# Attention of one layer: scores of stacked bf16 parts, computed a second time transposed and less their maximum, instead of transposed probabilities

## The chip, the cores and the metric

The kernel runs on one core of a Trainium2 chip. The metric is the device time of one execution in microseconds (us). The engines are PE (TensorE), DVE (VectorE), ACT (ScalarE), POOL (GpSimd) and SP, which issues DMAs; ACT issues some too.

## The reference

A gated cross attention and then a gated mixture of experts, for 16 batches of 128 rows of 256 features:

```
x = x + tanh(g_xattn) * xattn(layernorm(x), ctx, ctx)      # 16 heads of 16, causal
x = x + tanh(g_ffn) * experts(layernorm(x))                # 32 experts x 4 sets

Q, K, V = q @ Wq.T, k @ Wk.T, v @ Wv.T                     # split in heads
scores = where(causal, Q K^T, -inf) / sqrt(16)
out = (softmax(scores) V) @ Wo.T + bo

logits = grouped rows of 32 . controller, + ramp; perm = (logits == max over the rows)
out = perm^T (relu(perm rows . f1 + bias) . f2)
```

The factors on Wq and Wk make the scores large, and the routing compares for equality, so the attention is computed at nearly full float32 precision.

## The kernel before

Everything is in one program with hand-placed semaphores; each engine's instructions stand in the order in which its block writes them. There are three stages: attention over the 16 batches, routing (`route`) over the 16 batches, and the experts with the weighted return (`expert_in`, `expert_out`, `transpose_y`, `combine`).

In attention, a batch has four chunks of four heads (`HC` = 4, `NC` = 4), `attend` runs over them, and I call one chunk's turn on PE a slot. In a slot PE adds the causal mask in bf16 (L340) and the scores in float32 (L344), in four 32-column tiles of the array; weighs V with the transposed probabilities of three slots ago (L360, `weigh_v`); transposes the probabilities of two slots ago (L351, `transpose_p`); and does one piece of the projections: K (L320), the output rows (L330) with the transposes of x (L313), Q (L320), and V (L330). L330 multiplies a high and a low part in three products; L320 is plain float32, which PE executes as two passes. DVE takes the row maximum (L908), ACT the exponential per head with its sum (L673), DVE the reciprocal (L857), POOL scales the probabilities (L261), and ACT and DVE by turns copy the transposed probabilities (L638, L870). PE works two and three slots behind, so POOL's product is not waited for in the steady state. `bass.ds` and `Fori` are loops of the program; batches 3 to 14 are in them.

At the start DVE takes the statistics of the first four batches (L820), then 13 steps for the reciprocal deviation (`rstd`), and normalizes (L839). SP loads the context, x and the first 16 of 32 experts' weights (`wx`, a ring of `RING` = 16) before the loop; the other 16 are loaded while the experts run, each when a place is free.

## Time and profile before

| | us |
|---|---|
| median of 3 runs | 319.41 (316.90 to 321.29) |
| profiled execution | 319.98 |
| its span, first to last instruction | 318.2 |
| first scores on PE | 18.4 |
| last residual of attention | 203.5 |
| routing, to the first expert on PE | 237.2 |
| experts, to the first transpose of the return | 282.2 |

The stretches are read from the order of time of the instructions. 1.8 us of the execution lie outside the span. The profile gives a granted clock of PE as a share of 2.4 GHz: 1.00 is 2.4 GHz and 0.50 is 1.2 GHz. Lengths of single matmuls overlap, since they are pipelined; distances between their starts are what PE spends.

### The profile page before, as it was taken

The page shows a single profiled execution, that of the slowest core. Times are in us where ns is not written, and L with a number is a line of the kernel's source. Part 1 is how long each engine was busy: PE and PEld are TensorE (multiplying, and loading weights), DVE is VectorE, ACT ScalarE, POOL GpSimd, SP SyncE. Part 2 cuts the span into 40 slices and gives each one's busy share as a digit, 9 for nine tenths or more (in the row PEclk, how much of TensorE's full clock was granted, in tenths as well). Part 3 has the DMA queues.
Part 4 walks back from the last instruction along what each step waited for, and adds up shares of the span by engine and source line. Part 5 has one row for each costly group of instructions (what it writes and reads, how often), then busy time and mean ns, then how long its engine had stood idle before and what let it go on. Part 6 is the DMA issues. An engine that isn't in the chain of part 4 may idle for free.

```text
span 318.2 us, 9488 instructions
## 1 busy us (share of the span) xinstructions
PE 286.0 (90%) x3472; PEld 223.0 (70%) x3472; DVE 212.5 (67%) x531; ACT 190.8 (60%) x722; POOL 107.8 (34%) x140
## 2 busy tenths in 40 slices
PE   2195899999999999999999997789988899979995
PEld 2153667778887877777877766667767789867773
DVE  1965997988788887878787984899964233212222
ACT  2035677777777777777777785278764233234553
POOL 4114345544554554455445555145510000000000
PEclk9999999999999999999999997799999755559999
DMA  6992000000000000000000000000005640001222
GB/s 199 369 388 88 2 19 19 19 1 20 16 16 0 16 16 16 0 16 16 13 4 0 0 2 2 0 1 2 0 0 180 214 144 2 6 0 52 72 75 70
DMA packets 12362, 16.52 MB, mean 52 GB/s; under 512 B 1200, under 2 KB 7728, under 8 KB 12336
## 3 DMA queue, kind: packets, MB, share of 16 engines
q1 hardware_dynamic: 11472, 14.83, 14.2%
q10 hardware_dynamic: 864, 1.33, 1.3%
q8 instruction: 17, 0.28, 0.4%
q14 instruction: 9, 0.07, 0.1%
HBM read 14.06 MB, written 2.10 MB: 51 GB/s over the span
## 4 chain that ended last, share of the span: by engine, by line
PE 69%; DVE 13%; SPq 5%; issue 5%; DMA 3%; ACT 3%; POOL 1%; DVEq 0%; ACTq 0%; POOLq 0%
PE banks L351 10%; PE banks L344 9%; PE banks L360 9%; PE banks L562 8%; PE banks L590 7%; PE banks L320 7%; PE banks L330 7%; PE banks L545 4%; DMA cT<-in_ctxT_dram 3%; PE banks L599 3%; PE banks L340 3%; SPq L214 2%; DVE nmax L908 2%; DVE permb L897 2%; PE banks L520 1%
## 5 line engine op out<-in xcount | busy, mean ns | idle before, releaser
L673 ACT ACTIVATE pr<-banks,nmax 128x128 f32<-128x128 f32 x256 | 90.5, 369 | 24.0 <-PE banks L351 17.3
L261 POOL TENSOR_TENSOR pr<-pr,rsum 128x512 f32<-128x512 f32 x64 | 66.6, 1041 | 92.3 <-DVE rsum L857 92.1
L344 PE MATMUL banks<-kd,qz 128*32 128x128 f32 (+3 forms) x512 | 66.9, 437 | 0.0
L360 PE MATMUL banks<-pT,va 128*32 128x128 f32 x512 | 62.0, 276 | 1.7 <-ACT pT L638 1.3
L908 DVE TENSOR_REDUCE nmax<-banks 128x4 f32<-128x512 f32 x64 | 44.0, 687 | 19.5 <-PE banks L344 18.2
L673 ACT ACTIVATION_READ_ACCUMULATOR pr<-banks,nmax 128x1 f32 x256 | 53.2, 208 | 0.0
L360 PEld LDWEIGHTS banks<-pT,va 128*32 128x32 f32 x512 | 38.3, 110 | 17.5 <-DVE pT L870 2.6
L351 PE MATMUL banks<-cf,pr 128*128 128x128 f32 x256 | 42.4, 289 | 1.6 <-POOL pr L261 1.5
L351 PEld LDWEIGHTS banks<-cf,pr 128*128 128x128 f32 x256 | 27.1, 141 | 15.4 <-issue 11.5
L638 ACT ACTIVATE pT<-banks 128x512 f32<-128x512 f32 x32 | 19.2, 599 | 18.5 <-PE banks L351 18.5
L562 PE MATMUL banks<-hb,wx 32*128 32x64 f32 x512 | 27.4, 377 | 2.1 <-ACT hb L751 1.0
L562 PEld LDWEIGHTS banks<-hb,wx 32*128 32x128 f32 x512 | 24.9, 280 | 4.5 <-issue 2.6
L756 ACT ACTIVATE routed<-banks 128x512 f32<-128x512 f32 x16 | 9.6, 598 | 30.0 <-PE banks L562 30.0
L1042 DVE COPY routed<-banks 128x512 f32<-128x512 f32 x16 | 11.1, 692 | 23.8 <-PE banks L562 23.8
L772 ACT ACTIVATE ys<-banks 128x1024 f32<-128x1024 f32 x16 | 16.7, 1043 | 16.0 <-PE banks L590 16.0
L590 PEld LDWEIGHTS banks<-cf,routed 128*128 128x128 f32 x128 | 20.9, 251 | 7.2 <-issue 6.2
L1054 DVE SCALAR_TENSOR_TENSOR xs<-banks,tg,xs 128x256 f32<-128x256 f32 x16 | 7.7, 484 | 26.1 <-PE banks L599 26.1
L590 PE MATMUL banks<-cf,routed 128*128 128x128 f32 x128 | 24.0, 337 | 0.8 <-ACT routed L756 0.8
L320 PE MATMUL banks<-cT,w 128*128 128x128 f32 x128 | 18.5, 290 | 6.6 <-ACT cTh L645 6.0
L839 DVE TENSOR_SCALAR xn<-xs,mv,rs 128x256 f32 (+1 forms) x32 | 23.8, 743 | 0.0
L870 DVE COPY pT<-banks 128x512 f32<-128x512 f32 x32 | 22.0, 688 | 1.6
L320 PEld LDWEIGHTS banks<-cT,w 128*128 128x128 f32 x128 | 16.7, 204 | 8.4 <-DMA w<-in_wattn_dram 5.9
(89 smaller groups left out, 525.2 us busy)
## 6 DMA issues: line engine op xcount, KB each, us to landing
wx<-in_wexp_dram SPq DMA_DIRECT2D x32, 256.5 KB, 5.9
cT<-in_ctxT_dram SPq DMA_DIRECT2D x16, 128.0 KB, 2.1
xs<-in_x_dram SPq DMA_DIRECT2D x4, 512.0 KB, 10.7
out_dram<-xs SPq DMA_DIRECT2D x16, 128.0 KB, 1.7
w<-in_wattn_dram ACTq DMA_DIRECT2D x4, 256.0 KB, 8.0
cf<-in_constf_dram ACTq DMA_DIRECT2D x1, 148.0 KB, 5.9
gb<-in_gbo_dram ACTq DMA_DIRECT2D x1, 129.0 KB, 7.9
ctrl_in<-in_ctrl_dram SPq DMA_DIRECT2D x1, 128.0 KB, 10.5
```

The lines of the kernel that those rows point to most:

```text
L261: pool.tensor_tensor(pr[:, c % 2], pr[:, c % 2], rsum[:, c * HC:(c + 1) * HC, None].to_broadcast([P, HC, P]), ALU.mult)\
L320: last = pe.matmul(dst[:, o * P:(o + 1) * P], weight[:, i, o * P:(o + 1) * P], src[:, i, :], start=(i == 0), stop=(i == KH - 1))
L330: last = pe.matmul(dst[:, 0:E], stationary, moving, start=(q == 0), stop=(q == len(parts) - 1))
L344: last = pe.matmul(bs[r, :, 0:(j + 1) * DP], qz[:, k, c // 2, c % 2, r], kd[:, k, c // 2, :, 0:(j + 1) * DP], start=False, stop=True, tile ...
L351: last = pe.transpose(BT[:, j * P:(j + 1) * P], pr[:, c % 2, j, :], ident)
L360: last = pe.matmul(BO[k][j * DP:(j + 1) * DP, o:o + P], va[:, k, c * HC + j, D * (1 - odd):][:, 0:DP], pT[:, c % 2, j * P:(j + 1) * P], st ...
L562: last = pe.matmul(bank[4 + s][:, o:o + GROUPS], wx[s * F:(s + 1) * F, e % RING, KH * P + h * P:KH * P + (h + 1) * P], hb[s * F:(s + 1) * ...
L590: last = pe.transpose(BY2[k][g // 2][:, o:o + P], routed[:, h, :, b * NG + g], ident)
L673: last = act.activation(pr[:, c % 2, j, :], BS[c % 2][:, j * P:(j + 1) * P], ACT.Exp, bias=nmax[:, c * HC + j:c * HC + j + 1], accum_out=p ...
L839: dve.tensor_scalar(xn[:, k, :], xs[:, b, :], mv[:, b, 0:1], rs[:, bass.ds(b, 1)], ALU.subtract, ALU.mult).then_inc(ready, 1)
L870: dve.tensor_copy(pT[:, c % 2, :], BT[:, :]).then_inc(pT_ready_dve, 1)
L908: dve.tensor_reduce(nmax[:, c * HC:(c + 1) * HC], BS[c % 2][:, :].rearrange("p (j t) -> p j t", j=HC), AX_X, ALU.max, negate=True).then_in ...
```

## The change

Q and K are projected for two batches at a time (a group), each in three products of high and low parts, with the weights' columns reordered by dimension. Each result is split in three bf16 parts (ACT, DVE, ACT, POOL), written to DRAM (`keep_rows`), and read back by three DMAs (`stack`) as a stack of 96 rows per head, six combinations of parts, so that one bf16 matmul over 96 rows gives the scores. The scores are computed twice: once as before (`scores`), from which DVE takes the row maximum alone, and six slots later transposed (`scores_less_max`), with three more rows that hold the three bf16 parts of the negative maximum (`split_max`, `spread_max`, `place_max`, three small DMAs per batch) against rows of ones. ACT takes one exponential over 512 columns, and the result is already what `weigh_v` needs. The transposes, the scaling on POOL and the copies are gone; `weigh_v` also multiplies with ones, which gives the sums, and DVE divides afterwards (`weigh_out`). The mask is added by one 512-column bf16 matmul for each of the two kinds of scores. The program of attention and routing is written out without loops. The tiles of attention share their memory with `wx` and `routed`, so all 32 experts' weights are loaded after the last residual (`x1_ready`, NB). The experts' instructions are otherwise the same.

```diff
+            def keep_rows(rows, parts, g, mid, low, kept):
+                sp.wait_ge(mid, g + 1)
+                sp.wait_ge(low, g + 1)
+                sp.dma_start(rows[g].rearrange("t r c -> r t c"), parts[:, :, :]).then_inc(kept, 16)
+            def stack(st, rows, g, order, kept, stacked):
+                sp.wait_ge(kept, 16 * (g + 1))
+                if g >= STACKS:
+                    sp.wait_ge(t_done, 2 * NC * (g - STACKS + 1))
+                at = 0
+                for lo, hi in order:
+                    n = (hi - lo) * D
+                    sp.dma_start(st[at:at + n, g % STACKS].rearrange("p h b c -> p (h b c)"),
+                                 rows[g, lo:hi].rearrange("t (d h) c -> (t d) (h c)", d=D)).then_inc(stacked, 16)
+                    at += n
...
+            def stack_q(g):
+                stack(qst, q_rows, g, ((0, 3), (0, 2), (0, 1)), q_kept, q_stacked[g % STACKS])
+            def stack_k(g):
+                stack(kst, k_rows, g, ((0, 3), (1, 3), (2, 3)), k_kept, k_stacked[g % STACKS])
...
+            load_x(0)
+            load_context(0)
+            load_context(1)
+            for i in range(1, NB // XC):
+                load_x(i)
             sp.dma_start(ctrl_in[:, :, :], ctrl).then_inc(small_loaded, 16)
-            for r in range(RING):
-                sp.dma_start(wx[:, r], wexp[r]).then_inc(wx_loaded[r], 16)
-            with sp.Fori(1, NB // 2) as i:
-                b = i * 2
-                for k in range(2):
-                    sp.wait_ge(c_ready, b + (k - 1))
-                    sp.wait_ge(k_done, b + (k - 1))
-                    sp.dma_start(cT[:, k], ctxT[b + k]).then_inc(ctx_loaded[k], 16)
-            for e in range(RING, NE):
-                sp.wait_ge(e_done, (e - RING) // 2 + 1)
-                sp.dma_start(wx[:, e - RING], wexp[e]).then_inc(wx_loaded[e - RING], 16)
-            with sp.Fori(0, NB // 2) as i:
-                b = i * 2
-                for k in range(2):
-                    sp.wait_ge(yo_ready, b + (k + 1))
-                    sp.dma_start(out[b + k], xs[:, b + k, :]).then_inc(stored, 16)
+            keep_k(0)
+            stack_k(0)
+            load_context(2)
+            keep_q(0)
+            stack_q(0)
+            load_context(3)
+            keep_k(1)
+            keep_q(1)
+            stack_k(1)
+            stack_q(1)
+            for g in range(NG2):
+                if 1 <= g < NG2 - 1:
+                    keep_q(g + 1)
+                    stack_q(g + 1)
+                if g + 2 < NG2:
+                    keep_k(g + 2)
+                    stack_k(g + 2)
+                if g + 4 < NG2:
+                    load_context(g + 4)
+            sp.wait_ge(x1_ready, NB)
+            for e in range(NE):
+                sp.dma_start(wx[:, e], wexp[e]).then_inc(wx_loaded[e], 16)
...
+            pool.affine_select(causal.rearrange("p (j t) -> p j t", j=HC), causal.rearrange("p (j t) -> p j t", j=HC),
+                               [[0, HC], [-1, P]], ALU.is_ge, NEG, base=0, channel_multiplier=1)
+            pool.affine_select(causalT.rearrange("p (j q) -> p j q", j=HC), causalT.rearrange("p (j q) -> p j q", j=HC),
+                               [[0, HC], [1, P]], ALU.is_ge, NEG, base=0, channel_multiplier=-1)\
+                .then_inc(masks_ready, 1)
...
+            def project_k(g, o, to):
+                if o == 0:
+                    pe.wait_ge(c_ready, g + 1)
+                project(to, K, cTh[:, g % CR], cTl[:, g % CR], o, k_done if o == KH - 1 else None)
...
+                to = BS[n % 2]
+                pe.matmul(to[:, :], identb, causal, start=True, stop=False, skip_group_check=True)
+                for j, h in enumerate(idx):
+                    last = pe.matmul(to[:, j * P:(j + 1) * P], qst[0:SROWS, g % STACKS, h, b % 2, :],
+                                     kst[0:SROWS, g % STACKS, h, b % 2, :], start=False, stop=True,
+                                     skip_group_check=True)
                 last.then_inc(s_done, 1)
...
+            def scores_less_max(n):
...
+                    pe.wait_ge(rows_loaded[b % 2], 48 * (b // 2 + 1))
+                if n >= 2:
+                    pe.wait_ge(p_ready, n - 1)
+                to = BT[n % 2]
+                pe.matmul(to[:, :], identb, causalT, start=True, stop=False, skip_group_check=True)
+                for j, h in enumerate(idx):
+                    last = pe.matmul(to[:, j * P:(j + 1) * P], kst[0:TROWS, g % STACKS, h, b % 2, :],
+                                     qst[0:TROWS, g % STACKS, h, b % 2, :], start=False, stop=True,
+                                     skip_group_check=True)
+                last.then_inc(t_done, 1)
...
+            def spread_max(b):
+                pe.wait_ge(np_ready, b + 1)
+                if b >= 3:
+                    pe.wait_ge(x1_ready, b - 2)
+                pe.matmul(BB[0:PARTS * H, 0:P], npart[:, :, :].rearrange("p t h -> p (t h)"), identb,
+                          start=True, stop=True).then_inc(nT_done, 1)
...
+                pe.wait_ge(p_ready, n + 1)
+                window = slice(D * (1 - e), D * (1 - e) + DP)
+                for at, kind in ((0, "v"), (E, "ones")):
+                    for j in range(HC):
+                        left = va[:, b % VR, o * 8 + 4 * e + j, window] if kind == "v" else ones[:, window]
+                        last = pe.matmul(BO[b % 2][j * DP:(j + 1) * DP, at + o * P:at + (o + 1) * P], left,
+                                         pT[:, n % PR, j * P:(j + 1) * P], start=(e == 0 and at == 0), stop=(e == 1),
+                                         tile_position=(0, j * DP), skip_group_check=True)
                 last.then_inc(av_done, 1)
...
+            pe.wait_ge(w_low[K], 1)
+            for o in range(KH):
+                project_k(0, o, BA)
             pe.wait_ge(consts_loaded, 16)
-            pe.wait_ge(xn_ready, 1)
-            transpose_x(0, 0)
-            pe.wait_ge(w_loaded[1], 16)
-            pe.wait_ge(xT_ready, 1)
-            project(BQ, wq, xT, q_done)
-            pe.wait_ge(w_ready, 1)
-            pe.wait_ge(c_ready, 1)
-            pe.wait_ge(k_ready, 1)
...
+            for n in range(SLOTS_N):
+                s, g = n % 8, n // 8
+                if 0 <= n - LT < CH:
+                    if n == LT:
+                        pe.wait_ge(qr_ready, 2)
+                    scores_less_max(n - LT)
+                if n < CH:
+                    scores(n)
+                if s % 4 == 0 and 0 <= n // 4 - 1 < NB:
+                    if n == 4:
+                        pe.wait_ge(xTl_ready, 1)
+                    spread_max(n // 4 - 1)
+                if 0 <= n - LA < CH:
+                    weigh_v(n - LA)
+                if s in (1, 2) and g + 2 < NG2:
+                    if s == 1 and g >= 1:
+                        pe.wait_ge(qr_ready, g + 2)
+                    project_k(g + 2, s - 1, BA)
+                if s % 4 == 0 and 0 <= n // 4 - 1 < NB:
+                    project_v(n // 4 - 1)
+                if s == 4 and g + 2 < NG2:
+                    pe.wait_ge(kr_ready, g + 3)
+                    transpose_x(g + 2, BA)
+                if s % 4 == 2 and 0 <= (n - 14) // 4 < NB:
+                    project_out((n - 14) // 4)
+                if s in (6, 7) and g + 2 < NG2:
+                    project_q(g + 2, s - 6, BA)
+                if n == CH + 1:
+                    pe.wait_ge(max_ready, CH)
+                    transpose_r(0)
+                if n == CH + 3:
...
+            def weight_high(m):
+                act.wait_ge(w_loaded[m], 16)
+                if m in (K, Q):
+                    for j in range(2 * KH):
+                        last = act.activation(wh[:, m].rearrange("p k (o d h) -> p (k o) d h", o=KH, d=D)[:, j],
+                                              by_dim(w, m)[:, j], ACT.Copy)
+                else:
...
+            def mid_part(parts, rest, g, rest_ready, ready):
+                act.wait_ge(rest_ready, g + 1)
+                act.activation(parts[:, 1, :], rest[:, :], ACT.Copy).then_inc(ready, 1)
...
+                act.activation(pT[:, n % PR, :], BT[n % 2], ACT.Exp, scale=float(D) ** -0.5).then_inc(p_ready, 1)
+            def place_max(b):
+                act.wait_ge(nT_done, b + 1)
+                if b >= 2:
+                    act.wait_ge(rows_loaded[b % 2], 48 * (b // 2))
+                act.activation(nT[:, b % 2, :], BB[0:PARTS * H, 0:P], ACT.Copy).then_inc(nT_ready, 1)
+                act.wait_ge(nT_ready, b + 1)
+                for t in range(PARTS):
+                    act.dma_start(qst[SROWS + t:SROWS + t + 1, (b // 2) % STACKS, :, b % 2, :], nT[t * H:(t + 1) * H, b % 2, :])\
+                        .then_inc(rows_loaded[b % 2], 16)
...
+            context_high(0)
+            weight_high(K)
+            weight_high(Q)
+            k_high(0)
+            context_high(1)
+            k_mid(0)
+            xT_high(0, BB)
+            q_high(0, bank[4])
+            k_high(1, bank[5])
+            q_mid(0)
+            k_mid(1)
+            xT_high(1, bank[3])
+            weight_high(V)
+            q_high(1, bank[2])
+            q_mid(1)
+            act.wait_ge(gates_loaded, 16)
+            act.activation(tg[:, :], gates_sb[:, :], ACT.Tanh).then_inc(tanh_ready, 1)
+            context_high(2)
+            weight_high(WO)
...
+            dve.memset(kst[SROWS:TROWS], 1.0).then_inc(shift_ready, 1)
...
+            def split_max(b):
+                m, r = nmax[:, b % 2, :], nrest[:, b % 2, :]
+                dve.wait_ge(max_ready, NC * (b + 1))
+                if b >= 1:
+                    dve.wait_ge(nT_done, b)
+                dve.tensor_copy(npart[:, 0, :], m).then_inc(np_step, 1)
+                dve.wait_ge(np_step, 3 * b + 1)
+                dve.tensor_tensor(r, m, npart[:, 0, :], ALU.subtract).then_inc(np_step, 1)
+                dve.wait_ge(np_step, 3 * b + 2)
+                dve.tensor_copy(npart[:, 1, :], r).then_inc(np_step, 1)
+                dve.wait_ge(np_step, 3 * b + 3)
+                dve.tensor_tensor(npart[:, 2, :], r, npart[:, 1, :], ALU.subtract).then_inc(np_ready, 1)
...
+            def weigh_out(b):
+                dve.wait_ge(av_done, NC * (b + 1))
+                dve.reciprocal(rsum[:, :, :], BO[b % 2][:, E:2 * E].rearrange("p (h t) -> p h t", h=KH))\
+                    .then_inc(rsum_ready, 1)
+                dve.wait_ge(rsum_ready, b + 1)
+                if b >= 1:
+                    dve.wait_ge(onl_ready, b)
+                dve.tensor_tensor(on[:, :, :], BO[b % 2][:, 0:E].rearrange("p (h t) -> p h t", h=KH), rsum[:, :, :],
+                                  ALU.mult).then_inc(on_ready, 1)
...
+            normalize_x(0)
+            normalize_x(1)
+            weight_low(K)
+            weight_low(Q)
+            k_rest(0)
+            xT_low(0, BB)
+            normalize_x(2)
+            normalize_x(3)
+            q_rest(0, bank[4])
+            k_rest(1, bank[5])
+            xT_low(1, bank[3])
+            q_rest(1, bank[2])
             dve.wait_ge(gates_loaded, 16)
             dve.wait_ge(tanh_ready, 1)
             dve.tensor_scalar(bo_sb[:, :], bo_sb[:, :], tg[:, 0:1], None, ALU.mult).then_inc(bo_ready, 1)
-            split_weight(1)
-            attend(0, 0, first=True)
+            statistics(XC, NB)
+            for stage in range(RSTD_STAGES):
+                if stage == 0:
+                    rstd_ready()
...
+            for n in range(SLOTS_N):
+                s, g = n % 8, n // 8
+                if n < CH:
+                    row_max(n)
+                if s % 4 == 3 and n // 4 < NB:
+                    split_max(n // 4)
+                if s % 4 == 3 and 0 <= (n - 15) // 4 < NB:
+                    residual((n - 15) // 4)
+                if s == 0 and 2 <= g + 1 < NG2:
+                    q_rest(g + 1)
+                if s % 4 == 0 and 0 <= n // 4 - 3 < NB:
+                    weigh_out(n // 4 - 3)
+                if s in (1, 2) and g + 2 < NG2:
+                    normalize_x(2 * (g + 2) + s - 1)
+                if s == 3 and g + 2 < NG2:
+                    k_rest(g + 2)
+                if s == 5 and g + 2 < NG2:
+                    xT_low(g + 2)
+                if n == CH - 2:
+                    dve.wait_ge(stats_ready, late)
+                if CH - 2 <= n < CH + 2:
```

PE in the loop, in the steady state. Before, from the second slot of a batch to the next:

```order
L340 MATMUL banks<-cb 32x4x32 x4
L344 MATMUL banks<-kd,qz 32x4x32
L344 MATMUL banks<-kd,qz 32x4x64
L344 MATMUL banks<-kd,qz 32x4x96
L344 MATMUL banks<-kd,qz 32x512
L360 MATMUL banks<-pT,va 32x128 x4
L351 MATMUL banks<-cf,pr 128x128 x4
L320 MATMUL banks<-cT,w 128x128 x4
```

After, one slot (L504 and L506 are the scores less the maximum, L486 and L488 the plain scores, L534 `weigh_v`, L428 half of K's projection):

```order
L504 MATMUL banks<-cb 128x512
L506 MATMUL banks<-qst,kst 128x128 x4
L486 MATMUL banks<-cb 128x512
L488 MATMUL banks<-kst,qst 128x128 x4
L534 MATMUL banks<-pT,va 32x128 x4
L534 MATMUL banks<-pT,ones 32x128 x4
L428 MATMUL banks<-cTh,wh 128x256
L428 MATMUL banks<-cTl,wh 128x256
L428 MATMUL banks<-cTh,wl 128x256
L428 MATMUL banks<-cTh,wh 128x256
L428 MATMUL banks<-cTl,wh 128x256
L428 MATMUL banks<-cTh,wl 128x256
```

The transposes are gone, and the mask and the scores stand twice; `weigh_v` has twice the matmuls.

DVE at the start, after the last step of `rstd` for the first four batches (L839 normalizes, L908 is the first row maximum). Before:

```order
L839 TENSOR_SCALAR xn<-xs,mv,rs 128x256
L844 TENSOR_TENSOR kd<-banks,cf 128x512 x2
L853 COPY xT<-banks 128x256
L834 CAST wh<-w 128x512
L836 TENSOR_TENSOR wl<-w,wh 128x512
L839 TENSOR_SCALAR xn<-xs,mv,rs 128x256
L960 TENSOR_SCALAR gb<-gb,tg 128x256
L834 CAST wh<-w 128x512
L836 TENSOR_TENSOR wl<-w,wh 128x512
L908 TENSOR_REDUCE nmax<-banks 128x4
```

After (L995 sets the rows of ones, L998 normalizes, L1012 is the weights' low part, L1021, L1028 and L1033 are the rests of K, Q and x):

```order
L995 MEMSET kst 3x12288
L998 TENSOR_SCALAR xn<-xs,mv,rs 128x256 x2
L1012 TENSOR_TENSOR wl<-w,wh 128x128 x8
L1021 TENSOR_TENSOR kr<-banks,kp 128x512
L1033 TENSOR_TENSOR xTl<-banks,xTh 128x512
L998 TENSOR_SCALAR xn<-xs,mv,rs 128x256 x2
L1028 TENSOR_TENSOR qr<-banks,qp 128x512
L1021 TENSOR_TENSOR kr<-banks,kp 128x512
L1033 TENSOR_TENSOR xTl<-banks,xTh 128x512
L1028 TENSOR_TENSOR qr<-banks,qp 128x512
L1127 TENSOR_SCALAR gb<-gb,tg 128x256
L985 BN_STATS stats<-xs 128x6 x12
```

The memset and the splits now stand ahead of the first scores, and so do the statistics of the other twelve batches and a second round of `rstd`, which before lay between the chunks of the first batches; the first row maximum comes behind all of it.

## Rows read from the trace of the kernel before

**Rows 1.** The page, part 1: busy time, share of the span, instructions.

```profile
PE 286.0 (90%) x3472; PEld 223.0 (70%) x3472; DVE 212.5 (67%) x531; ACT 190.8 (60%) x722; POOL 107.8 (34%) x140
```

**Rows 2.** Windows, 31.7 to 183.3 us: busy time of each engine, clock, DMA.

```profile
31.70:183.30 151.60, 150.16 (x1763) 118.28 (x1763) 127.97 (x311) 114.78 (x531) 75.73 (x85) 1.00 0.04 11
```

**Rows 3.** Timeline of PE, one slot and two batch starts: start, length, line.

```profile
129.50 0.24 PE L340 MATMUL banks<-cb 128*32 128x128 bf16 x4
...
130.75 0.66 PE L351 MATMUL banks<-cf,pr 128*128 128x128 f32 x4
131.24 1.06 PE L320 MATMUL banks<-cT,w 128*128 128x128 f32 x8
...
140.25 0.24 PE L340 MATMUL banks<-cb 128*32 128x128 bf16 x4
```

**Rows 4.** Timeline of DVE, start of the program.

```profile
13.05 0.41 DVE L839 TENSOR_SCALAR xn<-xs,mv,rs 128x256 f32<-128x256 f32 x1
```

**Rows 5.** One line of the program, L825: duration ns min/median/max, forms.

```profile
L825 DVE MEMSET banks<- x2: 485/485/485, 1.0 to 1.5; 128x512 f32 x2
```

**Rows 6.** Groups of instructions, by line and form: busy us, mean ns.

```profile
L834 DVE CAST wh<-w 128x512 fp32r<-128x512 f32 x2 | 0.8, 416 | 0.0
L820 DVE BATCH_NORM_STATS2 stats<-xs 128x6 f32<-128x256 f32 x16 | 6.0, 412 | 6.1 <-DMA xs<-in_x_dram 6.1
L908 DVE TENSOR_REDUCE nmax<-banks 128x4 f32<-128x512 f32 x64 | 44.0, 687 | 19.5 <-PE banks L344 18.2
L638 ACT ACTIVATE pT<-banks 128x512 f32<-128x512 f32 x32 | 19.2, 599 | 18.5 <-PE banks L351 18.5
L261 POOL TENSOR_TENSOR pr<-pr,rsum 128x512 f32<-128x512 f32 x64 | 66.6, 1041 | 92.3 <-DVE rsum L857 92.1
```

**Rows 7.** Timeline of PE, the first projections and the first scores.

```profile
17.41 0.41 PE L330 MATMUL banks<-wl,cTh 128*128 128x256 f32 x1
17.63 0.41 PE L330 MATMUL banks<-wh,cTh 128*128 128x256 f32 x1
...
18.40 0.30 PE L340 MATMUL banks<-cb 128*32 128x128 bf16 x4
```

**Rows 8.** The page, part 6, DMA issues: KB each, median us to landing.

```profile
cT<-in_ctxT_dram SPq DMA_DIRECT2D x16, 128.0 KB, 2.1
```

**Rows 9.** Timeline of PE, 187 to 200 us.

```profile
187.24 0.28 PE L330 MATMUL banks<-wl,onTh 128*128 128x256 f32 x1
187.35 0.28 PE L330 MATMUL banks<-wh,onTh 128*128 128x256 f32 x1
...
199.12 0.43 PE L360 MATMUL banks<-pT,va 128*32 128x128 f32 x8
199.48 0.33 PE L384 MATMUL banks<-cf,pc 128*128 128x128 f32 x1
```

**Rows 10.** Timeline of ACT's queue, a DMA issue, and the page's transfer rate.

```profile
0.74 0.41 ACTq L615 DMA_DIRECT2D w<-in_wattn_dram  x1
...
GB/s 199 369 388 88 2 19 19 19 1 20 16 16 0 16 16 16 0 16 16 13 4 0 0 2 2 0 1 2 0 0 180 214 144 2 6 0 52 72 75 70
```

**Rows 11.** Timeline of DVE, the last residual.

```profile
202.98 0.48 DVE L866 SCALAR_TENSOR_TENSOR xs<-banks,tg,xs 128x256 f32<-128x256 f32 x1 [0.80 <-PE banks L330]
```

**Rows 12.** Timeline of PE and windows, expert stage.

```profile
240.39 1.12 PE L562 MATMUL banks<-hb,wx 32*128 32x64 f32 x32 [0.33 <-ACT hb L751]
242.42 1.12 PE L562 MATMUL banks<-hb,wx 32*128 32x64 f32 x32
...
247.45 0.43 PE L545 MATMUL banks<-routed,wx 128*32 128x64 f32 x16 [1.52 <-issue]
...
253.05 1.99 PE L562 MATMUL banks<-hb,wx 32*128 32x64 f32 x32
...
255.97 1.99 PE L562 MATMUL banks<-hb,wx 32*128 32x64 f32 x32
...
250.00:251.00 1.00, 1.00 (x24) 1.00 (x24) 0.00 (x0) 0.00 (x0) 0.00 (x0) 0.50 0.68 220
```

927 lines of the change are left out of this document (435 added, 492 removed).

## The prediction

> **What bounds the kernel now.** I read the page's first part: PE is busy for 286 of 318.2 us, DVE for 67%, ACT for 60%, POOL for 34% [rows 1]. That is a mean over stages, so next the windows: in the steady attention, 31.7 to 183.3 us, PE is busy for 150.2 of 151.6 us at full clock, DVE for 128.0, ACT for 114.8, POOL for 75.7 [rows 2]. The timeline of PE then gives the price of a batch: the mask of one batch's first slot stands at 129.50, the next batch's at 140.25, so 10.75 us a batch and 2.69 a slot [rows 3]. PE in order is the bound of attention. Taking work from POOL and ACT is worth nothing there by itself; only what PE issues counts, and what stands before PE's first scores and behind its last. Further on the experts run at half the clock from 250 us on [rows 12], which the change doesn't touch directly.
>
> **PE's slot, part by part.** Removed from a slot are the tiled mask and float32 scores with `weigh_v` beside them, 1.25 us (129.50 to 130.75), the four transposes with a change of the array's layout, 0.49 us (130.75 to 131.24), and plain float32 projections at eight passes for one of K or Q [rows 3].
>
> Added are these. Two masks of 512 bf16 columns: a matmul of 256 columns in one pass stands 0.11 us from the next [rows 9], 0.117 over a whole chain of six, so 512 cost 0.213. Eight bf16 matmuls of 128 columns with a fresh stationary each, whose price p no row shows: from below it is half of 0.107, 0.053; from above the four transposes, which load 128 columns and stream 128 in 0.49 us, 0.12 each [rows 3]. In those the load hides behind the stream altogether, and a bf16 load has half the bytes, so I take 0.07. `weigh_v` with 16 passes instead of 8: alone, 8 passes and the change of layout behind them take 0.36 us (199.12 to 199.48) [rows 9]; doubled, less one of two changes, 0.64. The projections: a group of two batches has 24 products for K and Q and 24 for V and the output, 48 at 0.117 are 5.6 us, with four transposes (0.45) and two small ones for the maximum (0.12) 6.2 us for 8 slots, 0.77 a slot. The sum is 2 x 0.213 + 8 x 0.07 + 0.64 + 0.77 = 2.40 us. So the steady slot falls by 0.29 us, 18 us over 64 slots. With p = 0.053 it is 2.26, with p = 0.12 it is 2.80, longer than now.
>
> The Trainium skill, "TensorE: Matmul & The Clock Gate", section "Back-to-back issue gap", gives some 81 ns per matmul for a sustained stream of loads and 128-column matmuls; by it, as an estimate, the sum below would be 5 us longer. No row here has that form.
>
> The other engines don't bind. ACT has one exponential of 512 columns, some 0.60 [rows 6], and in a group six copies of that size; with the rest 1.7 us a slot. DVE has a maximum (0.69), per group three rests at 0.69, four small steps twice, and `weigh_out`; 1.85 us a slot. POOL's scaling (1.04 each) gives way to three subtractions of that size per group [rows 6].
>
> **The start.** Today PE's first scores stand at 18.40 [rows 7]. In the new order DVE comes to the memset at 13.05, where it normalizes now [rows 4]. The memset is 12288 elements on three partitions. The row of a DVE memset has 485 ns for 512 elements, 0.95 ns each [rows 5], so 11.6 us; a copy between SBUF tiles takes 0.81 ns each [rows 6], which gives 10 us, and nothing shows whether bf16 goes two at a time, which would be 5 to 6. I take 11.6, since it is the same instruction: 24.7. The Trainium skill, "VectorE: DVE Perf Modes", section "Zero memsets can be issued as uint32 (trn2)", says that a memset takes a cycle per element whatever the type, an estimate of 12.8 us; the row agrees within a tenth, and the rule speaks against the change, since nothing hides this memset.
>
> Behind it stand two normalizations (0.41 each) and four strided subtractions for K's weights (some 0.28 each), so K's projection starts at 26.6. From there one chain: 12 products at 0.21, PE being cold as now at 17.4 to 17.6 [rows 7] (29.4), K's high part on ACT 0.6, its rest on DVE 0.7, middle part and x's high part on ACT behind a context copy 2.0, x's low part 0.7 (32.8 to 33.5), Q's projection 2.6 (to 36), high part, rest, K(1)'s projection and copy, middle part (39.2), low part on POOL 1.04 (40.3). Then the trip through DRAM: issue 0.5 (the issue of a 256 KB load is 0.41 [rows 10]), landing 2.1 or more [rows 8], three loads of 786 KB in all, 2.1 us at the 370 to 390 GB/s of the page [rows 10] and a landing. The stack is there at 47 or 48, and the first scores with it.
>
> DVE is later still: the rests of group 1 end at 44.5, 12 statistics at 0.41 [rows 6] and 13 steps of `rstd` as long as those from 9.6 to 13.05 give 53. Only then is the first row maximum taken. The four maxima of batch 0, two normalizations and `split_max` end at 58.2; the maximum's own trip (matmul, copy 0.3, three issues at up to 0.4, landing 2.1) ends at 61.7, where the first transposed scores start.
>
> **The sum.** Left for PE at 61.7 are 64 x (transposed scores) and 58 x (plain scores) = 122 x (0.213 + 4 x 0.07) = 60.1, `weigh_v` 64 x 0.64 = 41.0, K and Q of the remaining groups 17.7, V 10.5, output 11.2, the small matmuls 1.0: 141.5 us. Added: 2 for PE's clock at the ramp, 4 for the waits for the maximum in the steady state (below), 3.2 for the end, where reciprocal, product, high part, low part, projection and residual follow one another. So the last residual ends at 61.7 + 141.5 + 2 + 4 + 3.2 = 212.4, against 203.5 now (202.98 + 0.48) [rows 11]: +8.9.
>
> Behind it I leave the routing and the experts as they are, less 1 us for the loops that are written out. The experts' loads, 8.2 MB, now start there; at 370 GB/s they take 23 us, and routing takes 33.7 (203.5 to 237.2), so they are hidden; their cover would be gone only under half that rate. From the profiled execution, 319.98 + 8.9 - 1 = 327.9; I say 328. That execution is 0.6 us above the median of the three runs.
>
> **The wait for the maximum.** `scores_less_max` of a batch waits in its first slot for three rows that start from the plain scores of the batch's last slot, two slots ahead. Counted from the start of the slot in between: both kinds of scores 1.0, the small matmul 0.2, copy 0.4, three issues 0.2 to 1.2, landing 2.1: 3.9 to 4.9 us against two slots, 4.8. So 0 to 0.1 us a batch, and with the traffic of the stacks beside it some 0.25: 4 us in all. Queued behind that wait on PE are the next plain scores, `weigh_v` and a projection, and behind these DVE and ACT; no other work stands ahead of it.
>
> **Rivals.**
> 1. *The experts keep the full clock; not slower.* Today the granted clock falls at 249.9 to 0.50, that is 1.2 GHz, after PE stood for 1.52 us for its own instructions at 245.9 [rows 12], while the ring's second half of weights was being loaded at 144 to 214 GB/s [rows 10]. The change takes those loads out of this stage. If the wait was theirs and the fall came of it, a pair of experts takes 2.03 us (240.39 to 242.42) and not 2.92 (253.05 to 255.97) [rows 12]: 10 pairs give 9, the last pair and the first transposes 2, the wait 1.5: 12.5 us, so 315.5. Against it: PE has gaps there even at full clock, 0.33 us in a pair [rows 12], and the fall may come of those. It decides if no wait of over 1 us stands in the stage.
> 2. *The maximum misses its slots.* A landing of 3 us and issues of 0.4 beside the stacks' traffic give 1.25 us a batch instead of 0.25: 16 more, 344.
> 3. *The weight loads bind the bf16 matmuls*: p = 0.12, 488 x 0.05 = 24 more, 352.
> 4. *The start is shorter*: bf16 memset two at a time (-6) and quick trips through DRAM (-3): 319.
> 5. *All cheap*: p = 0.053 (-8), full clock (-12.5), a wait or two more: 310.
> That the change doesn't do what it says isn't one: the order shows the transposes gone.
>
> **Chances.** The forecast 0.30, rival 1 0.25, rival 2 0.15, rival 3 0.10, rival 4 0.12, rival 5 0.08. The range takes in all but rival 3 and the edges: 309 to 347. Over 2% is about what a measurement of this kernel tells from no change, 313.0 and 325.8 around the median. Faster: rival 5 and a third of rival 1, 0.16. Same: the rest of rival 1 and rival 4, 0.29. Slower: the forecast and rivals 2 and 3, 0.55.
>
> **What the changed profile would show.** The memset at 11 to 13 us on DVE, before any normalization; first scores at 45 to 50, first transposed ones at 59 to 64; slots of 2.3 to 2.5 us, PE busy for over 95% of the steady state and its idle time at the first slot of every batch, released by a DMA to `qst`; eight bf16 matmuls 0.06 to 0.08 apart; the last residual at 212; experts at 0.50 of the clock. I am wrong if PE's slot isn't its own work (DVE or ACT late, maxima late by over 1 us), if p is at an end of its range, if the start is off by more than 8 us, or if the clock of the experts stays.

## The result, and the profile after

The changed kernel takes **382.13 us** (median of 4 runs, 376.46 to 385.52) against 319.86 of the kernel before on the same chip: a ratio of 1.186, 95% interval 1.166 to 1.206, slower. The prediction was 328.0 with a range of 309 to 347; its sign was right, its size was not, and the time lies 35 us outside the range. The profiled execution is the fastest of the four, 376.46 us with a span of 374.7. The ratios leave out executions over 1.5% above the fastest of their kernel, so a version is compared with the changed kernel by the difference of the two ratios, times 319 us, and not by the medians.

The page of the changed kernel: busy times from its first part, the chain that ended last by engine from its fourth, and VectorE's reciprocal from its fifth.

```profile
PE 272.5 (73%) x3520; PEld 209.7 (56%) x3552; DVE 212.1 (57%) x461; ACT 138.4 (37%) x283; POOL 73.8 (20%) x103
...
PE 44%; DVE 21%; DMA 16%; issue 7%; ACTq 6%; ACT 5%; POOL 1%; DVEq 0%; SPq 0%
...
L1065 DVE RECIPROCAL rsum<-banks 128x256 f32<-128x256 f32 x16 | 27.9, 1747 | 0.0
```

PE did less than before (286.0 [rows 1]) in a longer time: the kernel waits. The windows view from the first transposed scores to the last residual, to be held against [rows 2]:

```profile
66.20:270.80 204.60, 157.88 (x1974) 118.49 (x2006) 120.74 (x237) 70.05 (x150) 43.63 (x54) 0.93 0.34 77
```

And the waits of PE in that stretch (total, times, longest):

```profile
PE banks L504 <- DMA qst<-nT: 25.6, 12, 4.1
PE banks L450 <- POOL onl L362: 6.5, 2, 4.4
PE banks L428 <- DVE qr L1028: 5.2, 5, 1.8
PE banks L517 <- DVE xs L1077: 4.2, 7, 1.0
```

Of 204.6 us PE stands for 46.7, and 25.6 of these are `scores_less_max` (L504) at a batch's first slot, waiting for the maximum's rows in `qst`. The granted clock of the stretch is 0.93 where it was 1.00, and it falls behind such waits. The windows over one of them (the wait of 3.80 us shown further down) and the time behind it:

```profile
191.00:195.00 4.00, 0.21 (x8) 0.00 (x0) 1.44 (x3) 1.30 (x4) 2.43 (x3) 1.00 0.47 109
...
196.00:198.00 2.00, 2.00 (x23) 1.42 (x21) 0.69 (x1) 0.26 (x1) 0.00 (x0) 0.50 0.30 102
```

The timeline of a slot of PE:

```profile
172.79 0.38 PE L486 MATMUL banks<-cb 128*128 128x512 bf16 x1
173.01 0.39 PE L488 MATMUL banks<-kst,qst 96*128 96x128 bf16 x4
173.32 0.43 PE L534 MATMUL banks<-pT,va 128*32 128x128 f32 x8
...
173.90 0.38 PE L428 MATMUL banks<-xTh,wh 128*128 128x256 f32 x1
174.71 0.39 PE L504 MATMUL banks<-cb 128*128 128x512 bf16 x1
174.94 0.39 PE L506 MATMUL banks<-qst,kst 99*128 99x128 bf16 x4
175.16 0.38 PE L486 MATMUL banks<-cb 128*128 128x512 bf16 x1
```

The mask takes 0.22 us (172.79 to 173.01), `weigh_v` 0.58 (173.32 to 173.90), four bf16 matmuls 0.22 (174.94 to 175.16), which is p = 0.055. The mask is at its term (0.213), the other two are under theirs (0.64 and 0.07).

Then the trip of the maximum, twice. First an odd batch, in the timeline of PE, ScalarE and the queues:

```profile
186.02 0.39 PE L504 MATMUL banks<-cb 128*128 128x512 bf16 x1
...
187.62 0.22 PE L517 MATMUL banks<-cb,npart 128*48 128x128 bf16 x1 [0.54 <-DVE xs L1077]
...
187.88 0.27 ACT L823 ACTIVATE nT<-banks 48x128 bf16<-48x128 f32 x1 [0.60 <-PE banks L517]
188.18 1.79 ACTq L826 DMA_DIRECT2D qst<-nT  x3
...
187.83 1.23 SPq L272 DMA_DIRECT2D qst<-q_rows  x3
...
195.01 0.39 PE L504 MATMUL banks<-cb 128*128 128x512 bf16 x1 [3.80 <-DMA qst<-nT]
```

The DMAs issued from 187 to 190 us (KB each, us from issue to landing):

```profile
qst<-q_rows SPq DMA_DIRECT2D x1, 128.0 KB, 6.0
qst<-nT ACTq DMA_DIRECT2D x3, 4.0 KB, 5.4
```

The three small DMAs are issued in 1.79 us and land 5.4 us (median) after their issue, beside three reads of a stack that SyncE issued at the same moment; PE has stood for 3.80 us when they are there. In the even batch ahead of it no stack is read at that moment; its timeline:

```profile
176.28 2.44 ACTq L826 DMA_DIRECT2D qst<-nT  x3
178.82 0.60 ACT L774 ACTIVATE qp<-banks 128x512 bf16<-128x512 f32 x1 [2.58 <-issue]
...
180.19 0.39 PE L428 MATMUL banks<-cTh,wh 128*128 128x256 f32 x1 [1.31 <-DVE qr L1028]
```

And its DMAs:

```profile
qst<-nT ACTq DMA_DIRECT2D x3, 4.0 KB, 2.5
```

They land after 2.5 us and in time, but the issues hold ScalarE for 2.44 us, `q_high` behind them comes late, `q_rest` behind that, and PE's next projection has waited 1.31 us for `qr`.

The start in the timelines of VectorE and PE, and the last residual, to be held against [rows 4], [rows 7] and [rows 11]:

```profile
15.65 10.30 DVE L995 MEMSET kst<- 3x12288 bf16 x1 [2.62 <-issue]
...
27.87 0.58 PE L428 MATMUL banks<-cTh,wh 128*128 128x256 f32 x1 [27.87 <-DVE wl L1012]
...
53.27 0.63 PE L488 MATMUL banks<-kst,qst 96*128 96x128 bf16 x4 [8.46 <-POOL ctrl_sb L387]
...
55.99 1.29 DVE L1041 TENSOR_REDUCE nmax<-banks 128x4 f32<-128x512 f32 x2
...
66.45 0.39 PE L506 MATMUL banks<-qst,kst 99*128 99x128 bf16 x4 [0.66 <-DMA qst<-nT]
...
270.35 0.48 DVE L1077 SCALAR_TENSOR_TENSOR xs<-banks,tg,xs 128x256 f32<-128x256 f32 x1 [3.05 <-PE banks L450]
```

And the windows view in the experts' stage, where [rows 12] had a clock of 0.50:

```profile
310.00:320.00 10.00, 8.74 (x324) 7.59 (x321) 4.60 (x10) 4.05 (x10) 0.00 (x0) 1.00 0.02 5
320.00:330.00 10.00, 8.86 (x311) 7.57 (x315) 4.40 (x9) 3.99 (x9) 0.00 (x0) 1.00 0.02 4
```

At the end of the stage the clock falls here too: it is 0.71 from 334 to 338 us and 0.50 from 338 to 342.

From the last residual's end to the end of the execution are 105.6 us (376.46 - 270.83), where the kernel before has 116.5 (319.98 - 203.46). So the 48.6 us between the forecast (327.9) and the profiled execution (376.46) are +4.5 at the start (first transposed scores at 66.2 instead of 61.7), +53.9 from there to the last residual (204.6 instead of 150.7) and -9.9 behind it.

### The profile page after: what moved, and what is told of

Read it like the earlier page. It is cut to its first block, busy times and chain, and to the rows that moved or that the text cites. A ratio compares the mean times of both kernels' runs of the same rounds, so it can differ in the third digit from the quotient of the medians.

```text
span 374.7 us, 8661 instructions
## 1 busy us (share of the span) xinstructions
PE 272.5 (73%) x3520; PEld 209.7 (56%) x3552; DVE 212.1 (57%) x461; ACT 138.4 (37%) x283; POOL 73.8 (20%) x103
## 4 chain that ended last, share of the span: by engine, by line
PE 44%; DVE 21%; DMA 16%; issue 7%; ACTq 6%; ACT 5%; POOL 1%; DVEq 0%; SPq 0%
DMA qst<-nT 13%; PE banks L428 7%; PE banks L711 6%; ACTq L826 6%; PE banks L683 5%; PE banks L450 5%; PE banks L534 3%; PE banks L506 3%; DVE kst L995 3%; PE banks L488 3%; PE banks L486 2%; PE banks L647 2%; DVE rsum L1065 2%; PE banks L720 2%; PE banks L504 2%
## 5 line engine op out<-in xcount | busy, mean ns | idle before, releaser
L815 ACT ACTIVATE pT<-banks 128x512 f32<-128x512 f32 x64 | 38.0, 593 | 73.3 <-PE banks L506 73.3
L428 PE MATMUL banks<-cTh,wh 128*128 128x256 f32 x32 | 12.1, 378 | 33.0 <-DVE wl L1012 27.9
L488 PE MATMUL banks<-kst,qst 96*128 96x128 bf16 x256 | 27.4, 234 | 8.5 <-POOL ctrl_sb L387 8.5
L504 PE MATMUL banks<-cb 128*128 128x512 bf16 x33 | 13.5, 409 | 25.6 <-DMA qst<-nT 25.6
L534 PE MATMUL banks<-pT,va 128*32 128x128 f32 x512 | 28.4, 295 | 0.0
L506 PE MATMUL banks<-qst,kst 99*128 99x128 bf16 x256 | 26.1, 226 | 3.0 <-DMA qst<-nT 0.7
L1065 DVE RECIPROCAL rsum<-banks 128x256 f32<-128x256 f32 x16 | 27.9, 1747 | 0.0
L428 PEld LDWEIGHTS banks<-cTh,wh 128*128 128x128 f32 x32 | 7.7, 240 | 35.4 <-DVE wl L1012 27.9
L534 PE MATMUL banks<-pT,ones 128*32 128x128 f32 x512 | 27.0, 284 | 0.0
L488 PEld LDWEIGHTS banks<-kst,qst 96*128 96x128 bf16 x256 | 21.8, 106 | 9.2 <-issue 2.5
L486 PE MATMUL banks<-cb 128*128 128x512 bf16 x63 | 26.1, 415 | 0.6 <-DVE nmax L1041 0.6
L506 PEld LDWEIGHTS banks<-qst,kst 99*128 99x128 bf16 x256 | 20.8, 101 | 8.4 <-issue 1.4
L504 PEld LDWEIGHTS banks<-cb 128*128 128x128 bf16 x64 | 6.3, 98 | 32.9 <-DMA qst<-nT 28.6
```

What stands on the lines that cost most here:

```text
L428: last = pe.matmul(to[:, o * E:(o + 1) * E], stationary, moving, start=(q == 0), stop=(q == len(parts) - 1))
L486: pe.matmul(to[:, :], identb, causal, start=True, stop=False, skip_group_check=True)
L488: last = pe.matmul(to[:, j * P:(j + 1) * P], qst[0:SROWS, g % STACKS, h, b % 2, :], kst[0:SROWS, g % STACKS, h, b % 2, :], start=False, st ...
L504: pe.matmul(to[:, :], identb, causalT, start=True, stop=False, skip_group_check=True)
L506: last = pe.matmul(to[:, j * P:(j + 1) * P], kst[0:TROWS, g % STACKS, h, b % 2, :], qst[0:TROWS, g % STACKS, h, b % 2, :], start=False, st ...
L534: last = pe.matmul(BO[b % 2][j * DP:(j + 1) * DP, at + o * P:at + (o + 1) * P], left, pT[:, n % PR, j * P:(j + 1) * P], start=(e == 0 and ...
```

## The experiments

Each number is a median in us, with the ratio to the kernel before in brackets; that kernel took 318.6 to 319.9 in these comparisons.

### Is it the maximum's trip?

**No trip.** The rows of the maximum are filled once with a constant, the DMAs and the waits for them are gone.

```diff
-                for t in range(PARTS):
-                    act.dma_start(qst[SROWS + t:...], nT[t * H:(t + 1) * H, b % 2, :]).then_inc(rows_loaded[b % 2], 16)
...
+            pool.memset(qst[SROWS:TROWS], -32.0).then_inc(ones_ready, 1)
```

> Leaves out the three small DMAs that carry the row maximum to qst, and PE's wait for them; the three rows hold a constant, so the probabilities are not the reference's. Everything else, the copy nT included, stays. Theory A (the trip of the maximum bounds attention: ACT's three issues of 0.5 to 1.3 us each and a landing of up to 5.6 us): a group of two batches falls from about 28 us to the 19 to 21 us of PE's own work, so the time falls by 50 to 60 us, to 320 to 330. Theory B (DVE bounds it, with a reciprocal of 1.75 us a batch that I had put at 0.45): under 10 us less, 370 or more. Theory C (PE's lower clock in attention costs it): only as the waits go, clock back to 1.00, and most of the gain would show as shorter matmuls.

Measured **332.8** (1.041, 1.032 to 1.049): 47 us less than the changed kernel by the ratios and 43 between the two profiled executions, a little above theory A's 320 to 330. The window from the first transposed scores to the last residual, and in a second view PE's waits in it:

```profile
65.20:227.80 162.60, 148.19 (x1977) 112.52 (x2007) 120.87 (x237) 69.46 (x151) 42.35 (x52) 0.97 0.42 94
```

```profile
PE banks L453 <- POOL onl L362: 4.9, 2, 4.4
PE banks L518 <- DVE xs L1071: 4.8, 8, 1.0
```

The stretch is 42.0 us shorter: idle time falls by 32.3 (46.7 to 14.4) and busy time by 9.7, with the clock at 0.97 instead of 0.93. The waits for `qr` went with those for the rows, since nothing holds ScalarE any more.

**One part.** The maximum is rounded to one bf16 part (any shift cancels in the quotient), so one row and one DMA go where three did.

```diff
-                for t in range(PARTS):
+                for t in range(MP):                      # MP = 1, TROWS = SROWS + MP
                     act.dma_start(qst[SROWS + t:...], ...)
```

> The shift is the maximum rounded to one bf16 part instead of three, in both numerator and sum, so softmax is the same up to rounding: one DMA per batch and not three, one small step on DVE and not four. Theory A: two issues on ACT (1.2 to 1.9 us) and 0.6 us of DVE steps leave each batch's chain, 1.5 to 2.5 us a batch where it waits: 25 to 35 us less, 345 to 355. Theory B: only the 0.6 us on DVE, 10 us less at most, 370.

Measured **352.2** (347.1 to 354.1): 30 us less, as expected.

**One issue.** All three parts, but sent by one DMA.

```diff
-                for t in range(PARTS):
-                    act.dma_start(qst[SROWS + t:SROWS + t + 1, ...], nT[t * H:(t + 1) * H, b % 2, :])
+                act.dma_start(qst[SROWS:TROWS, ...], nT[:, b % 2, :])
```

> The changed kernel with the maximum's three parts written by one DMA instead of three (same bytes, same three rows of 16 x 128). ScalarE then issues once, some 0.6 us, where its three issues took 1.8 to 2.6. If the issues on ScalarE's queue make up a good part of the trip (theory I), a batch gains 1.2 to 2 us, 19 to 32 in all: 350 to 363 us, near the 352 of the kernel with one part. If it is the landing beside the stacks' reads (theory L), which one DMA of the same bytes meets as three do: 370 to 380.

Measured **361.0** (1.131, 1.118 to 1.145): 18 us less than the changed kernel, a little under theory I's 19 to 32, with the time in its range. In the timeline of ScalarE's queue one issue takes 0.74 us where three took 1.79 and 2.44:

```profile
178.63 0.74 ACTq L825 DMA_DIRECT2D qst<-nT  x1
```

**Lighter stacks.** From the fourth group on, only the first of the three reads of a stack is made, so the lower parts of scores are stale.

```diff
-                for lo, hi in order:
+                for lo, hi in (order if g < STACKS else order[:1]):
```

> For groups 3 to 7 each stack is loaded by the first of its three DMAs alone (48 of 96 rows; the others keep old values, so scores are wrong): half of the stack traffic from there on. Theory A with contention (the maximum's DMAs land after 4.2 to 5.6 us in the batches in which a stack is being read, 1.2 us in the others): 1.5 to 3 us less in five odd batches, 8 to 15 us less, 365 to 373. If the landing is slow of itself: no change, 380.

Measured **369.0** (1.150, 1.137 to 1.163): some 12 us less. PE's waits for the rows fall from 25.6 us to

```profile
PE banks L504 <- DMA qst<-nT: 17.3, 10, 2.9
```

So the stacks' reads make up part of the landing. Half of the reads in five of eight groups were worth 12 us and two of three issues in every batch 18; which of the two is the larger part of the whole trip isn't shown.

**More lead, first try.** The transposed scores and `weigh_v` go two slots later and nothing else moves; one wait of PE is added, for the copy of V ahead of the maximum's small matmul.

```diff
-LT = 6
-LA = 8
+LT = 8
+LA = 10
```

> LT = 8 and LA = 10 instead of 6 and 8: the transposed scores come eight slots behind the plain ones, so the maximum has four slots instead of two; with one wait more on PE for the copy of V ahead of spread_max, needed for order on the bank. All DMAs stay. Theory A: the wait at the first slot of a batch is gone, what is left is ACT's issue time ahead of q_high (1 to 2 us a group): 40 to 50 us less, 330 to 340, with 1 to 2 us more at the end. Theory B: no gain, 375 to 385.

Measured **375.9** (365.7 to 377.9), some gain at best, and not the 330 to 340 of theory A. The waits of PE say why:

```profile
PE banks L450 <- POOL onl L362: 23.3, 11, 3.7
```

No wait for the rows is left in the list; 23.3 us for `onl` stand in its place. `weigh_v` of a batch now ended two slots later, while the output's projection kept its slot, so reciprocal, product, high part and low part no longer fit ahead of it. The edit had moved the wait, and told nothing against the trip.

**More lead, whole.** One slot more, and V's projection and the whole chain of the output one slot later too, with the same added wait.

```diff
-LT = 6
-LA = 8
+LT = 7
+LA = 9
...
-                if s % 4 == 2 and 0 <= (n - 14) // 4 < NB:
-                    project_out((n - 14) // 4)
+                if s % 4 == 3 and 0 <= (n - 15) // 4 < NB:
+                    project_out((n - 15) // 4)
```

> The changed kernel with the transposed scores and weigh_v one slot later behind the plain scores (LT 7, LA 9) and, other than in the run before with more lead, everything behind them one slot later too: V's projection, the reciprocal, the output's high part, low part and projection; so no step of the output's chain loses the distance it had. Theory A, the maximum's trip is what costs: one slot more (2.4 us) covers more than half of the waits of 1 to 4 us that stand once a batch, the chain of the output keeps its two slots, and the time comes to 345 to 360 us (with the trip wholly gone it was 333). Rival, the trip isn't what binds but whatever stands next to it in the engines' order (ScalarE's and VectorE's turns): the waits move to another line again, as with more lead alone, and the time stays at 368 to 382.

Measured **349.7** (1.097, 1.082 to 1.112): 28 us less, with a trip nearly as long as before (issues of 1.8 to 2.5 us, a landing of 2.9 in the median, where the changed kernel has 1.8 to 3.0 and 3.2). The waits of PE:

```profile
PE banks L428 <- DVE qr L1030: 8.3, 5, 2.0
...
PE banks L504 <- DMA qst<-nT: 2.2, 4, 1.5
```

25.6 us of waits for the rows became 2.2. It is the length of the trip against the two slots that it had, and not the traffic as such. What is left first of all is `qr`, the wait that went with the issues in the run without the trip.

**The reciprocal.** Replaced by a copy, so the quotient is not formed.

```diff
-                dve.reciprocal(rsum[:, :, :], BO[b % 2][:, E:2 * E]...)
+                dve.tensor_copy(rsum[:, :, :], BO[b % 2][:, E:2 * E]...)
```

> The changed kernel with the reciprocal of the 16 output steps replaced by a plain copy (so the attention's sums are multiplied in where they should be divided out, and the output is not the reference's). The copy should take 0.3 to 0.5 us where the reciprocal's row has 1.75, so VectorE has some 21 us less work. Theory A, the maximum's trip sets the batch: VectorE waits anyway, the step lies beside TensorE's wait for the rows, and the time stays within 2%, 370 to 382 us. Rival, VectorE's own work sets the batch (it delays the row maxima or the rests behind it): 12 to 20 us less, 357 to 369 us.

Measured **373.5** (1.156, 1.144 to 1.169): by the ratio some 10 us less for 21 of VectorE's work, between theory A's range and the rival's. VectorE's own work isn't the main bound, but the reciprocal isn't wholly beside the path either.

### The start

**Memset on GpSimd.**

```diff
+            pool.memset(kst[SROWS:TROWS]...bitcast(F32), ONES2).then_inc(shift_ready, 1)   # GpSimd, ahead of context_low(0)
-            dve.memset(kst[SROWS:TROWS], 1.0).then_inc(shift_ready, 1)
```

> The changed kernel with the memset of the stack's rows of ones moved from VectorE's head (10.30 us there, before any normalization) to GpSimd's, behind the masks and ahead of the first context's low part, as half as many float32 elements. Theory A, the memset stands on the start's path: the first K projection starts 9 to 12 us sooner (27.9 goes to 16 to 19) and the whole kernel takes 362 to 369 us. Rival, the path at the start is another one (GpSimd, which now has the memset and makes the copy of the control weights for which TensorE waited 8.5 us ahead of the first scores): the K projection starts sooner, the first scores don't, and the time stays within 1%, 372 to 381 us.

Measured **366.0** (1.139, 1.127 to 1.150), as theory A has it. GpSimd's memset in the timeline, and then PE's first wait and the one ahead of the first scores:

```profile
5.29 5.21 POOL L379 MEMSET kst<- 3x6144 f32 x1
```

```profile
PE banks L434 <- DVE wl L1017: 15.7, 1, 15.7
PE banks L492 <- POOL ctrl_sb L393: 8.1, 1, 8.1
```

The first K projection waits for 15.7 us instead of 27.9, and the span is 11.0 us shorter (363.7 against 374.7): the memset was on the path, and with it went the 2.62 us in which VectorE had stood ahead of it (now the first normalization follows the last step of `rstd` at once, 13.79 behind 13.59).

**Statistics behind the first maxima,** on top of that.

```diff
-            pe.wait_ge(ctrl_ready, 1)          # now ahead of the first logits
...
+                if n == 4:
+                    statistics(XC, NB)         # and the 13 steps of rstd, normalize_x(4), normalize_x(5)
```

> The kernel with the memset on GpSimd, with two more edits at the start: TensorE waits for the control weights ahead of the first logits instead of ahead of the first scores, and VectorE takes the 12 statistics and their rstd (7.7 us) behind the first batch's maxima instead of ahead of them. Theory B, the first transposed scores hang on VectorE's queue and on that wait, 8.1 us in the profile of the kernel with the memset moved: they come 5 to 9 us sooner, and the time is 356 to 362 us. Rival, the stack through DRAM isn't there any sooner than the wait ended, or the statistics now delay the maxima of batch 1: within 2 us of the 366 of the kernel with the memset moved alone.

Measured **369.4** (1.164, 1.150 to 1.177): no gain but some loss (a span of 366.4 us against 363.7), nearest to the rival. The waits of PE:

```profile
PE banks L426 <- DVE xn L1003: 7.0, 1, 7.0
...
PE banks L494 <- DMA qst<-q_rows: 6.0, 1, 6.0
```

Two things are read from it. The 8.1 us put down to the control weights were 1.6 of their own: without that wait the first scores came at 39.2 instead of 40.8, since the stack's landing ended 6.0 us of wait there. And the statistics, moved behind the maxima, were waited for by x's transposes.

### The experts' clock

**Loads again.** 16 loads of 256 KB are made beside the experts of the changed kernel, in the places of the ring's second half.

```diff
+            for e in range(16, NE):
+                sp.wait_ge(e_done, (e - 16) // 2 + 1)
+                sp.dma_start(wx[:, e - 16], wexp[e]).then_inc(again, 16)
```

> The changed kernel with 16 loads of 256 KB added in the experts' stage, issued on the sync queue in the same places as the ring's second half in the kernel before (weights of pairs that are done are loaded once more over themselves by others; they are not used again). Theory R, the loads beside the experts' matmuls cost TensorE its full clock: the experts' stage falls to a granted clock near 0.50 again and the time rises by 9 to 13 us, 384 to 396. Rival, the clock fell for want of weights or because of what stands ahead of the experts: no change beyond 1.5%, 374 to 384, and the clock of the stage stays at 0.9 or more.

Measured **392.2** (1.222, 1.213 to 1.231), 11 us more. Windows of the experts' stage (the last columns are clock, DMA share and GB/s):

```profile
320.00:330.00 10.00, 8.67 (x229) 7.67 (x219) 3.51 (x8) 3.12 (x8) 0.00 (x0) 0.69 0.66 205
340.00:350.00 10.00, 10.00 (x232) 8.96 (x225) 3.71 (x8) 3.41 (x8) 0.00 (x0) 0.50 0.01 3
```

PE waits for none of these loads, so a want of weights can't have stopped it: the loads went with the fall, and the clock stayed at 0.50 when they were over. The other executions of this kernel have mean clocks of 0.87 to 0.88, all four of the changed kernel 0.90 to 0.91. But PE did stand still ahead of this fall, which came at about 323.7 us, as it did in the kernel before (1.52 us [rows 12]). Both times it waited for nothing that the profile shows, which the profile calls `issue` and the prediction PE's own instructions:

```profile
323.03 0.43 PE L671 MATMUL banks<-routed,wx 128*32 128x64 f32 x16 [1.00 <-issue]
```

In the versions without loads there, the longest such wait in this stage is 0.6 us. So whether the loads cost the clock directly or through this wait isn't told apart by any run.

**The kernel before, second half of the ring not loaded** (experts 16 to 31 use the weights of 0 to 15).

```diff
-            for e in range(RING, NE):
-                sp.wait_ge(e_done, (e - RING) // 2 + 1)
-                sp.dma_start(wx[:, e - RING], wexp[e]).then_inc(wx_loaded[e - RING], 16)
```

> The kernel before without the second half of the ring's loads: experts 16 to 31 compute with the weights of experts 0 to 15, so the output is not the reference's. Theory R, the loads (or the wait for them) cost the clock: the stage keeps 1.0 of the clock, and the kernel takes 306 to 311 us instead of 319. Rival, the fall comes of the gaps in the pairs themselves: it stays at 0.50 from about the same place and the time at 317 to 321.

Measured **310.6** (0.971, 0.966 to 0.976), theory R. The window of 240 to 260 us has the clock at 1.00:

```profile
240.00:260.00 20.00, 17.98 (x640) 15.46 (x640) 8.93 (x19) 8.02 (x20) 0.00 (x0) 1.00 0.02 4
```

**The kernel before with the change's layout of SBUF alone.** The attention's tensors are given back once it is done, and all 32 experts are loaded behind the last residual.

```diff
-        w = sb("w", [P, 4, KH, E])                  # and the attention's other tensors
+        w = sb_att("w", [P, 4, KH, E])
...
+        early.close()
+        wx = sb("wx", [P, NE, KH * P + E + 1])
...
+            sp.wait_ge(x1_ready, NB)
+            for e in range(NE):
+                sp.dma_start(wx[:, e], wexp[e]).then_inc(wx_loaded[e], 16)
```

> The kernel before with one part of the change alone: the attention's tensors are closed once the attention is done, the 32 experts' weights lie in their place, and all 32 loads are issued behind the last residual, so none is left for the experts' stage. Nothing of the computation is left out. Theory R, the loads beside the experts' matmuls cost TensorE its full clock: the stage keeps 1.0 of it and the time is 308 to 313 us, as in the run in which the second half of the ring wasn't loaded (310.6). Rival, 8.2 MB behind the last residual delay the routing or the first experts, or the stage's clock falls all the same: 316 us or more.

Measured **305.8** (0.957, 0.952 to 0.963), the fastest of all versions, with nothing of the computation left out. Its windows, the first over the loads behind the last residual:

```profile
203.00:232.00 29.00, 26.32 (x196) 19.51 (x196) 25.01 (x67) 20.82 (x50) 11.95 (x24) 1.00 0.67 250
...
240.00:260.00 20.00, 17.61 (x620) 15.09 (x621) 8.64 (x20) 7.71 (x19) 0.00 (x0) 1.00 0.02 4
```

The first row says one thing more: beside the routing's matmuls 250 GB/s of loads left the clock at 1.00. So loads alone aren't enough for a fall; what the experts' stage adds isn't shown.

### Together

**Four edits of the changed kernel:** one part, one slot more for all, the memset on GpSimd, and the start of the run above (their diffs stand there).

> Four edits of the changed kernel together: the maximum in one bf16 part and one row (one DMA), everything behind the plain scores one slot later, the memset on GpSimd, the start's waits as in the run beside it. If the losses are the ones named (maximum's trip 49 us, start 16 and 5 to 9) and add up: from 352 with one part, 10 to 20 for the slot and 20 to 25 for the start, 307 to 322 us, which is the time of the kernel before or a little less. Rival, they overlap or another wait takes their place: 325 to 340.

Measured **328.3** (1.031, 1.022 to 1.041), above the 307 to 322 of the sum and in the rival's range. The largest waits of PE behind its first:

```profile
PE banks L427 <- DVE xn L1006: 8.8, 1, 8.8
PE banks L435 <- DVE xTl L1041: 8.5, 7, 2.8
```

**The same with two places of VectorE's order changed,** and then the same with three parts in one DMA.

```diff
-            statistics(XC, NB)
+            statistics(XC, 2 * XC)             # the last eight batches in slots 8 to 16
...
+                if s == 5 and g + 2 < NG2:     # moved ahead of weigh_out
+                    xT_low(g + 2)
```

> The four edits together (one part, one slot later, memset on GpSimd, control weights waited for at the logits), with two places of VectorE's order changed: the statistics ahead of the first maxima are only those of batches 4 to 7 (some 5 us), beside the wait for the stack's landing, and those of the last eight follow in slots 8 to 16; and x's low part goes ahead of the reciprocal, behind which it stood in slot 5. Theory S, what was left is VectorE's order: TensorE's wait of 8.8 us for xn at the start falls under 2 us, its 7 waits for x's low part (8.5 us with the one at the start) fall to the start's alone, and the time comes from 328 to 314 to 319 us, the kernel before within 2%. Rival, the trip through DRAM of the first stacks and of the first maximum binds at the start whatever VectorE does: 322 to 328.

> The same as the kernel beside it with the maximum in three bf16 parts again, sent in one DMA. With the slot of lead, theory A has the longer trip (three more small steps on VectorE, 0.6 us, and 12 KB instead of 4) hidden: within 3 us of the kernel with one part. Rival, the lead of one slot is used up by it: 4 to 10 us longer.

The first measured **321.9** (1.011, 1.002 to 1.019), 6.4 us less than the run above: theory S's signs are there (the wait for `xn` at the start is gone, those for x's low part fell to 6.2 us), its size is not, and the time lies at the lower edge of the rival's 322 to 328. The second, with three parts, has a median of **325.5** and a ratio of 1.010 (1.002 to 1.018), the same as with one part, as its theory A has it. What remained at the start is the stack's trip, as the rival said:

```profile
PE banks L493 <- DMA qst<-q_rows: 7.6, 1, 7.6
```

## Why the prediction was wrong, point by point

**The step that failed is "The wait for the maximum"**: "3.9 to 4.9 us against two slots, 4.8 ... some 0.25: 4 us in all". PE waited 25.6 us for the rows, and the trip cost over 40. For the odd batch shown, the trip takes 8.9 us from the start of the slot in between (L504 at 186.02) to the last landing (194.96), in four parts:

- both kinds of scores, and a wait for the residual of an earlier batch, whose bank the small matmul shares: 1.60 (1.0 in the sum, which has no such wait);
- matmul and copy: 0.56 (0.6);
- the issues up to the start of the last: 1.18 (0.2 to 1.2);
- from there to the landing: 5.60, where the sum had 2.1.

In the even batch the landing was short (1.81, from 178.11 to 179.92), but the three issues ran for 2.44. The 2.1 was the landing of a lone context load in an idle queue [rows 8]; beside a stack's reads no row of before could show it. The trip was taken away (-47 us), shortened (-30 and -18) and covered (-28), and each took its share of the time with it. Rival 2 had this mechanism, with 1.25 us a batch and a chance of 0.15; its price was some two fifths of what was found (47 us over 16 batches are 2.9). It counted only the wait: it left out what the issues hold up on ScalarE (5.2 us of waits for `qr`) and that PE is granted less of its clock behind its waits (most of the 9.7 us of busy time, as an estimate from 0.93 against 0.97). Without the trip the stretch is still 11.9 us longer than forecast (162.6 against 150.7): 4.8 are waits for the residual ahead of the small matmul and 2.3 one for `xn`, neither with a term in the sum, and the rest wasn't taken apart.

The Trainium skill, "DMA: Bandwidth & Descriptors", section "Queues, rings and completion order", has each DMA engine take turns between the queues that have work, a packet at a time; by that alone small transfers on ScalarE's queue should pass a bulk read on SyncE's at little cost. The trace agrees in part at most: 5.4 us beside the reads, 2.5 without them.

**PE's slot** was right in sum. p was 0.055 to 0.057 (0.07 taken, 0.053 the lower end), the mask 0.22 (0.213), `weigh_v` 0.58 (0.64). With the trip gone a group of two batches took 20.1 us, 2.51 a slot, of which 0.54 us a group is the wait for the residual: 2.45 against 2.40 forecast. That the sum fits is partly luck: the cheap terms are offset by dearer ones, a chain of six products at 0.81 (173.90 to 174.71) for 6 x 0.117 = 0.70, and the plain scores at 0.31 up to `weigh_v` (173.01 to 173.32) for 4 x 0.07 = 0.28. The figure of the Trainium skill, "TensorE: Matmul & The Clock Gate", section "Back-to-back issue gap", 81 ns for such a pair, is above what this trace has (four in 0.22 us, 55 ns each).

**The start**: the memset had 10.30 us (11.6 taken, 12.8 in the estimate beside it), but began at 15.65 and not at 13.05, behind 2.62 us in which VectorE waited for nothing that the profile shows; K's projection stood at 27.87 (26.6 taken). The queries' trip through DRAM was too short too: from the issue of `keep_q` at 41.11 to the first scores at 52.87 are 11.8 us, with the end of the wait for the control weights in it, where 7 to 8 were taken (9.4 in the kernel with four edits, 29.90 to 39.3, where no such wait lies on it). But the first row maximum didn't hang on these scores: VectorE came to it straight from `rstd` (the last step at 55.78, the maximum at 55.99). Its queue was late because the rests of group 1 ended at 46.3 (44.5) and the output's bias with its wait took 2.0 us that had no term; the statistics and `rstd` were 0.8 shorter than taken. So the first row maximum stands at 56.0 (53), the first transposed scores at 66.2 (61.7): 4.5 in all.

**The other engines don't bind** held in the main (VectorE was busy for 120.7 of 204.6 us), though a run without the reciprocal was some 10 us shorter, and `weigh_out`, which had no price of its own, was the dear step: 1.75 us for the reciprocal of 256 elements. The Trainium skill, "VectorE: DVE Perf Modes", section "First, the fixed hardware budget", says that a reciprocal is an iterative division with a repeat count of 8; the trace agrees in kind, 6.8 ns an element against 1.6 for the product of the same shape (0.42 us).

**The rest** was rival 1 (chance 0.25), which came true beside a failed main step: behind the last residual the profiled execution is 9.9 us shorter than forecast, where it expected 12.5. Its sign holds: no wait of over 1 us stands in the stage (the longest is 0.9). That the loads are its condition is shown by three runs; whether through PE's wait of over 1 us, as the rival had it, or directly isn't shown.

**The loads hidden behind routing** held: the kernel before with all 32 of them there is the fastest of all.

Why no edit of the changed kernel wins: in the best of them the attention ends at 214.1 us of 318.9, where that of before ends at 203.5. The slots are cheaper by some 0.2 us, 13 us in all, and the start is later by more than that: its first scores stand at 39.2 us, those of before at 18.4 [rows 7]. The remaining gain is the experts', and that is to be had without the transposed scores. How much of the 20 us at the start could still be taken back isn't known.

## What to carry to other kernels

A small DMA inside a loop is priced by its issue on the issuing engine, by its landing beside whatever else moves at that moment, and by who stands behind both; none of that is in the row of a lone load, and if it isn't known, give it slots until nothing waits. When a chain gets more lead, move everything that hangs on its end by as much, or the wait only changes its name. And try the parts of a change alone: here the layout of SBUF, a side matter of the change, was worth 4%, and the rest of the change lost more than that even in its best form, which has this layout too and stands at 1.010.

## What the runs showed of the hardware

- Three DMA issues in a row on ScalarE's queue, 4 KB each, took 1.8 to 3.0 us, one for the same 12 KB 0.73 to 0.76 in all batches but the first (1.36).
- Three such DMAs landed 5.4 us after their issue (median of one batch) beside 768 KB of reads issued on SyncE's queue at the same moment, and 2.5 us in a batch without them.
- A memset of 12288 bf16 on three partitions took 10.30 us on VectorE, 0.84 ns an element; the same bytes as 6144 float32 on GpSimd 5.21 us, 0.85 ns an element. So bf16 didn't go two at a time on VectorE; float32 at this length wasn't timed there.
- With 205 GB/s of loads beside them, and behind a wait of PE of 1.00 us for nothing that the profile shows, the experts' matmuls went from a granted clock of 1.00 to 0.50, which is 1.2 GHz, and stayed there after the loads. Without such loads two windows of the changed kernel and those of 240 to 260 us of two versions of the kernel before had 1.00. Beside the routing's matmuls 250 GB/s of loads left it at 1.00.
- Behind a wait of PE of 3.80 us in attention the granted clock was 0.50 from 196 to 198 us, and 1.00 again from 200 on.
